# A Strassen-like mixing kernel on one core: z12's sum and parts, and the splits of S1 and S2, in another order

## The reference

```python
# x: (128, 64, 1024), cond_128: (128, 128)
h = gelu(cond @ W0 + b0); h = gelu(h @ W1 + b1)
att = softmax(h @ W2 + b2)                      # (128, 8)
agg_w = einsum('bk,koi->boi', att, weight)      # a 64x64 matrix for each batch
agg_b = att @ bias_k
c = einsum('boi,bih->boh', agg_w, x) + agg_b[:, :, None]
# c flattened to 8192 rows of 1024
probs = softmax(c @ W_router.T)                 # 8 experts
topk_probs, topk_idx = top_k(probs, 2); topk_probs /= topk_probs.sum(-1)
hA = einsum('nd,erd->ner', c, A)                # rank 16 for each expert
expert_out = einsum('ner,eor->no', hA * combine, B) * 2.0
out = x + c @ W_base.T + b_base + expert_out
```

## Time and profile before

| | before |
|---|---|
| median of 3 runs | 1030.17 us |
| profiled execution | 1032.57 us |
| its span | 1030.6 us |
| TensorE busy | 963.7 us |
| VectorE busy | 830.4 us |
| ScalarE busy | 399.7 us |
| GpSimd busy | 437.9 us |
| DMA moved | 112.45 MB, 109 GB/s on average |

### The profile page before, as it was taken

One profiled execution on the slowest core, in us unless ns is written; L12 is line 12 of the kernel. 1 busy time (PEld: TensorE's weight loads), 2 busy tenths in 40 slices (PEclk: granted clock), 3 DMA queues, 4 the chain that ended last, 5 costly groups with the idle time before them and its releaser, 6 DMA issues.

```text
span 1030.6 us, 19700 instructions
## 1 busy us (share of the span) xinstructions
PE 963.7 (94%) x6697; PEld 941.9 (91%) x6697; DVE 830.4 (81%) x1496; ACT 399.7 (39%) x791; POOL 437.9 (42%) x326
## 2 busy tenths in 40 slices
PE   6869999999999999999999999999999999999996
PEld 5869999999999999999999999999999999999995
DVE  4888888887887888887788888788888888878873
ACT  4443344334234334334433423433433343343341
POOL 0143444443443544344444444354534445443452
PEclk9989999999999999999999999999999999999998
DMA  5523322223322123332222332222333222233312
GB/s 201 198 99 126 117 91 87 101 103 125 125 104 103 64 104 124 125 125 90 90 90 103 125 125 106 102 69 116 107 125 125 103 89 78 103 125 125 117 50 81
DMA packets 35084, 112.45 MB, mean 109 GB/s; under 512 B 13024, under 2 KB 13280, under 8 KB 30464
## 3 DMA queue, kind: packets, MB, share of 16 engines
q1 hardware_dynamic: 35072, 112.29, 30.2%
HBM read 76.56 MB, written 35.65 MB: 109 GB/s over the span
## 4 chain that ended last, share of the span: by engine, by line
PE 77%; DVE 14%; issue 4%; ACT 3%; DMA 1%; DVEq 0%; ACTq 0%
PE ps L384 19%; PE ps L382 19%; PE ps L386 19%; PE ps L430 9%; DVE x_lo L786 6%; PE ps L407 4%; PE ps L408 3%; PE ps L409 3%; DVE sum L805 2%; DVE z_lo L814 2%; ACT z_hi L591 2%; DVE w_lo L876 1%; PE ps L443 1%; DMA w_stage<-in_wide 1%; ACT w_hi L603 1%
## 5 line engine op out<-in xcount | busy, mean ns | idle before, releaser
L382 PE MATMUL ps<-w_hi,x_hi 128*128 128x290 f32 x1792 | 540.5, 302 | 11.8 <-DVE w_lo L876 7.6
L384 PE MATMUL ps<-w_lo,x_hi 128*128 128x290 f32 x1792 | 535.7, 299 | 0.0
L386 PE MATMUL ps<-w_hi,x_lo 128*128 128x290 f32 x1792 | 533.7, 298 | 0.0
L382 PEld LDWEIGHTS ps<-w_hi,x_hi 128*128 128x128 f32 x1792 | 341.0, 190 | 15.4 <-issue 11.9
L386 PEld LDWEIGHTS ps<-w_hi,x_lo 128*128 128x128 f32 x1792 | 341.3, 190 | 0.0
L384 PEld LDWEIGHTS ps<-w_lo,x_hi 128*128 128x128 f32 x1792 | 341.1, 190 | 0.0
L765 POOL TENSOR_TENSOR x_sb<-x_sb,row_bias 128x512 f32<-128x512 f32 x128 | 201.4, 1573 | 272.3 <-ACT row_bias L571 272.3
L760 POOL TENSOR_TENSOR x_sb<-x_sb,bias_out 128x512 f32<-128x512 f32 x128 | 193.4, 1531 | 191.0 <-DMA x_sb<-in_x 191.0
L786 DVE TENSOR_TENSOR x_lo<-xT_sb,x_hi 128x512 fp32r<-128x512 f32 x192 | 206.8, 1079 | 56.4 <-ACT x_hi L559 56.4
L559 ACT CAST x_hi<-xT_sb 128x512 fp32r<-128x512 f32 x192 | 118.6, 619 | 246.1 <-DVE xT_sb L802 211.3
L407 PE MATMUL ps<-z_hi,mix_hi 128*128 128x388 f32 (+1 forms) x192 | 69.0, 359 | 38.1 <-DVE z_lo L814 36.5
(11 more groups left out here) (85 smaller groups left out, 970.2 us busy)
## 6 DMA issues: line engine op xcount, KB each, us to landing
x_sb<-in_x SPq DMA_DIRECT2D x64, 512.0 KB, 4.5
result<-x_sb SPq DMA_DIRECT2D x64, 512.0 KB, 2.7
xT_sb<-in_xT SPq DMA_DIRECT2D x31, 1024.0 KB, 4.8
w_stage<-in_wide SPq DMA_DIRECT2D x3, 1160.0 KB, 6.7
agg_w_rows<-agg_w SPq DMA_DIRECT2D x1, 2048.0 KB, 8.7
mix<-agg_w_rows SPq DMA_DIRECT2D x124, 16.0 KB, 2.2
w_stage<-in_wide SPq DMA_DIRECT2D x2, 580.0 KB, 7.4
b_stage<-in_wide SPq DMA_DIRECT2D x1, 1160.0 KB, 13.6
```

Source lines behind the costliest of these rows:

```text
L382: nc.tensor.matmul(dst, x_hi[:, s, rows], w_hi[:, w, c, cols], start=first, stop=False, skip_group_check=True)
L384: nc.tensor.matmul(dst, x_hi[:, s, rows], w_lo[:, w, c, cols], start=False, stop=False, skip_group_check=True)
L386: mm = nc.tensor.matmul(dst, x_lo[:, s, rows], w_hi[:, w, c, cols], start=False, stop=last, skip_group_check=True)
```

## The change

The instructions of a unit stay the same; the order on VectorE and ScalarE changes.

- VectorE: the low parts of S2 and S1 of unit u+1 are made at the end of unit u, not in unit u; S4 is made right after z22's low part; S3's low part comes ahead of sum1, S4's low part between sum1 and `result(u-1, 0)`; z11's low part ahead of `hwT_low(u-1, 1)`; S1 of unit u+1 ahead of sum3; A11's low part ahead of `result(u-1, 1)`; S2 between sum2 and z12's low part.
- ScalarE: the casts of S2 and S1 of unit u+1 come last in unit u, behind a wait for A22's product (they stood behind z21's cast); A22's cast comes ahead of the save of sum2; z11's cast and the row bias ahead of the save of sum3; the wait for S4's product ahead of A12's cast goes.
- The part before the loop is changed likewise for unit 1. TensorE, GpSimd and SP keep their programs.

```diff
 # ScalarE, before the loop
+            act.wait_ge(s_made, 4 + SUM_AT["S2"])
+            act.wait_ge(product_mm, FIRST_AT["A22"])
             wait_row_bias_free(0, 0, 1)
+            x_high("S2")
+            x_high("S1")
             bias_of(0, 0, 1)
 
             def unit(u, par, last):
                 a, b = accumulators(par)
                 z21_high(u - 1, b)
-                act.wait_ge(s_made, u * 4 + SUM_AT["S2"])
-                x_high("S2")
-                x_high("S1")
                 z22_high(u - 1)
                 gate(u - 1, 0)
...
                 act.wait_ge(product_mm, count(u, "S2"))
+                x_high("A22")
                 save(sum2, a, u2_saved)
-                x_high("A22")
                 act.wait_ge(mixed_mm, tile_no(u - 1, 1) + 1)
                 mix_high(u, 1)
                 gate(u - 1, 1)
+                wait_row_bias_free(u, 0, 0)
+                z11_high(u)
+                bias_of(u, 0, 0)
                 act.wait_ge(product_mm, count(u, "S1"))
                 save(sum3, b, p5_saved)
                 hwT_high(u - 1, 1)
-                wait_row_bias_free(u, 0, 0)
-                z11_high(u)
-                bias_of(u, 0, 0)
...
                     x_high("A11")
-                if last:
-                    wait_row_bias_free(u, 0, 1)
                     z12_high(u)
-                else:
-                    z12_high(u)
-                    act.wait_ge(product_mm, count(u, "S4"))
                     wait_row_bias_free(u, 0, 1)
                     x_high("A12")
-                bias_of(u, 0, 1)
+                    bias_of(u, 0, 1)
+                    act.wait_ge(s_made, u * 4 + (4 + SUM_AT["S2"]))
+                    act.wait_ge(product_mm, count(u, "A22"))
+                    x_high("S2")
+                    x_high("S1")
 # VectorE
             make_s2(1)
+            x_low(1, "S2")
+            x_low(1, "S1")
 
             def unit(u, par, last):
                 a, b = accumulators(par)
                 z21_low(u - 1, b)
                 route(u - 1, 0)
-                x_low(u, "S2")
                 z22_low(u - 1)
+                dve.wait_ge(x_lo_done, count(u, "S2"))
+                make_s4(u)
                 hwT_low(u - 1, 0)
-                x_low(u, "S1")
+                x_low(u, "S3")
                 dve.wait_ge(p1_saved, u + 1)
                 dve.wait_ge(product_mm, count(u, "A12"))
                 add_acc(sum1, b, z11_summed)
+                x_low(u, "S4")
                 result(u - 1, 0)
-                x_low(u, "S3")
-                dve.wait_ge(x_lo_done, count(u, "A12"))
-                make_s4(u)
-                x_low(u, "S4")
                 x_low(u, "A22")
                 route(u - 1, 1)
+                z11_low(u)
                 hwT_low(u - 1, 1)
-                z11_low(u)
+                if not last:
+                    dve.wait_ge(xT_in, u * 16 + 16)
+                    make_s1(u + 1)
                 dve.wait_ge(p5_saved, u + 1)
                 dve.wait_ge(product_mm, count(u, "S3"))
                 add_acc(sum3, a, z22_summed)
+                if not last:
+                    x_low(u + 1, "A11")
                 result(u - 1, 1)
                 if not last:
-                    dve.wait_ge(xT_in, u * 16 + 16)
-                    make_s1(u + 1)
                     make_s3(u + 1)
-                    x_low(u + 1, "A11")
                 dve.wait_ge(u2_saved, u + 1)
                 dve.wait_ge(product_mm, count(u, "S4"))
                 add_acc(sum2, b, z12_summed)
+                if not last:
+                    dve.wait_ge(x_lo_done, count(u + 1, "A11"))
+                    make_s2(u + 1)
                 z12_low(u)
                 if not last:
                     x_low(u + 1, "A12")
-                    dve.wait_ge(x_lo_done, count(u + 1, "A11"))
-                    make_s2(u + 1)
+                    x_low(u + 1, "S2")
+                    x_low(u + 1, "S1")
```

More of the change, by code:

```diff
@@ L715, in unit @@
                 hwT_high(u - 1, 1)
-                wait_row_bias_free(u, 0, 0)
-                z11_high(u)
-                bias_of(u, 0, 0)
-                if not last:
+                if last:
+                    wait_row_bias_free(u, 0, 1)
+                    z12_high(u)
+                    bias_of(u, 0, 1)
+                else:
                     act.wait_ge(xT_in, u * 16 + 16)
```

## The result

| | before | after |
|---|---|---|
| median | 1030.03 us (4 runs, 1028.03 to 1030.34) | 989.64 us (4 runs, 989.04 to 991.17) |
| span of the profiled execution | 1030.6 us | 987.5 us |
| TensorE, VectorE, ScalarE, GpSimd busy | 963.7, 830.4, 399.7, 437.9 us | 957.9, 745.9, 415.3, 426.6 us |

The ratio is 0.9614, with a 95% interval of 0.9597 to 0.9631: faster by 40.4 us. The forecast was 997.0 in a range of 988 to 1014.

A forecast was written before the change was run, and what follows sets the result against it. TensorE, busy 94%, was taken to bound the kernel, its one repeated wait being for z12's low part. The terms -41.6 + 8.1 + 0.3 = -33.2 us took the median of 1030.17 to 997.0, range 988 to 1014.

The forecast's parts named there:

- z12's stall, 41.6 us: `mix_upper`: TensorE waits for z12's low part in 30 units; the reordering removes the whole stall, 41.6 us.
- step (c): End of the unit: z12's sum, S2, then z12's low part ending at 522.95, early by 1.15 us.
- rival 2: `mix_upper`: z12 later still, as S2 and z12's low part each lose the port to an addition; 1043.5 us, 7%.
- (d): First half of the unit: S4's low part ahead of `result(u-1, 0)` makes `mix_lower` 0.16 late, costing 0.26 us a unit.
- z22's and S4's places, "as before": First half of the unit: z22's part and S4 replace S2's and z22's parts, still two operations of 1.8 us.
- `mix_lower`, +8.1 us: `mix_lower`: S4's low part delays `result(u-1, 0)`, costing 0.26 us a unit in 31 units, 8.1 us.
- Rival 4: `mix_lower` isn't late at all, because S4's part finds a hole in front of it; 989 us, 5%.
- Once, +0.3 us: Prologue: casts of S2 and S1 start z21's first cast about 0.3 us later, between 0 and 1.2.
- VectorE first at S4's low part, by 0.3 us: Ahead of `result(u-1, 0)`: VectorE starts S4's low part 0.3 us before GpSimd's addition, so it pays nothing.
- rival 1: GpSimd is first in front of S4's low part; `mix_lower` stalls 1.36 us a unit; 1031.1 us, 6%.
- rival 3: Opening: S1's low part gets behind an addition, z21's low part is 0.8 us late; 25 us more, 1022, 8%.
- (a), (b): End of the unit: xT's load issued 2 us earlier, the x load 1.8 us earlier; GpSimd starts at 515.9.

The follow-up runs named there:

- e1: Changed kernel with S4's low part moved behind `result(u-1, 0)`: 981.28 us, ratio to the kernel before 0.9524.
- e2: Changed kernel with S4's cast ahead of the wait for GpSimd's addition and a 1-column copy behind it, so GpSimd's next addition starts first: 1022.43 us, ratio 0.9919.
- e4: Changed kernel with z12's low part ahead of the making of the next unit's S2: 997.53 us, ratio 0.967, on another chip.
- e5: Changed kernel with the next unit's S1 made behind `result(u-1, 1)` and ahead of S3: 997.43 us, ratio 0.9673, on another chip.
- e6: Kernel before with one move only, A11's low part of unit u+1 behind z12's low part: 997.34 us, ratio 0.9676.
- e3: Changed kernel with the casts and low parts of S2 and S1 back at the start of the unit: 1059.91 us, ratio 1.0288.

## Why the prediction was right

The forecast was a gain of 33.2 us; it was 40.4. The direction and the steps held; some sizes were off, and one effect was left out.

- **z12's stall, 41.6 us.** It is gone entirely, and z12's low part ends 26.87 us into the unit, within 0.01 of where step (c) put it (522.95 - 496.09). S2, in front of it, takes 0.68 us, so rival 2 did not come. But the term was mis-sized. A stalled unit pays the late start and, on top, 0.10 us because the first matmul behind a stall is longer; I put that on the new stall in (d) and not on the old one in the sum. The stage shrinks by 1.491 us, 44.7 us in 30 units: 3.1 more.
- **z22's and S4's places, "as before".** I gave the first half no gain, and held that TensorE's list of waits shows all there is to gain. It gained 0.090 us in the experts' stage, 2.7 us. In 19 of the first 30 units of before, S2 at the end of the unit took 1.81 us and not 0.69, the second of the races in the earlier trace rows; z21's low part then starts 1.03 to 1.04 us into the unit and not 0.94 to 0.96, and hwT's low part is 0.15 late. The weight load's waits for hwT's low part, 19 of up to 0.2 us (under the table of stages), are these. With S2 ahead of z12's low part, no addition is ready beside it, and S2 takes a median of 0.68 us.
- **`mix_lower`, +8.1 us.** Its mechanism is what the profile and e1 show: predicted 0.26 us a unit, measured 0.29 (0.220 + 0.073), which e1 gives back. Rival 4's time, 989, was met by coincidence and not by its cause: `mix_lower` is late in all 31 units, and it is the 3.1 and 2.7 us of the two points above, with 1.1 at the last unit and the end, that make up for it.
- **Once, +0.3 us.** In the first unit of the changed kernel z21's low part starts 0.99 us in and the experts' stage takes 1.47, for 0.95 and 1.43 before: 0.05 us, not 0.3.
- **VectorE first at S4's low part, by 0.3 us.** It is 0.28. e2 shows what the 0.28 is worth: 1022, as against the 1031 of rival 1; most of the difference is the 3.1 and the 2.7 us of above and 1.1 us of the last unit and the end. The Trainium skill's rule (SBUF — State Buffer, Who interferes with whom), that the first holds the shared port for its whole instruction, agrees with the two pairs of durations of e2 (1.29 and 1.69) and of the changed kernel (0.68 and 1.55), and a shared rate is excluded: the one that is first takes as long as alone.
- **The opening's 0.3 us to spare, rival 3.** It held in the changed kernel (z21's low part starts 0.87 us into the next unit, behind an idle of 0.20). e4, e5 and e6 use it up. In e4 and e5 the unit is 0.28 and 0.18 longer (29.35 and 29.26): 8.4 and 5.5 us in 30 units. The rest of the distance between their profiled executions and the changed kernel's is outside these units: e5's first unit starts 1.0 later, e4's last unit is 0.3 longer, and at the kernel's end the granted clock stays at 0.50 for 19.4 and 13.7 us and not for 6.8, 2.1 us in each; e6 loses 0.41 x 30 = 12 us of its gain. This was the right rival to look at, and its price of one whole addition an upper end.
- **(a), (b).** The x load lets GpSimd start 19.93 us into the unit for 19.8 predicted; xT's load is issued 13.64 us in, 1.9 us earlier than before.

Left open: 0.014 us of the opening stage, and why the granted clock comes back earlier at the kernel's end in one profiled execution than in another, which no run isolates.

## What to carry to other kernels

When one engine is dense, write down for each wait of it the reserve in front of it, not only the waits that exist: here 0.50 us before `mix_lower` and about 0.3 us at the opening decided 8 to 70 us, while the only long wait in TensorE's list was another. Count a stall's price between the starts of the instructions around it, in both the kernel with it and the one without it, and by the same rule. And put an operation that may run late behind the one that frees a resource (e1), even if both engines' totals stay the same.

## What the runs showed that I had not expected

- The list of waits can hide a stall: 0.29 us in each of 31 units stood in no row of TensorE's waits, but in the weight load's, as "issue", and in the distances between starts. The same holds for the 19 waits for hwT's low part in before.
- One 128x512 addition on GpSimd takes 1.29 us alone and one such operation on VectorE 0.68; started 0.16 to 0.28 us apart, the second takes 1.55 to 1.69. Started within 0.03 us of each other, either could win, in the same kernel, so that in before the same stage ran in two lengths (1.41 and 1.55 to 1.60).
- In e3, where TensorE waits 2.0 us in every unit, its granted clock fell to 0.50 behind this wait in five of 31 units, and each such unit is 1.5 us longer.
